# A sandwich layer on one core: expert outputs normalized in small groups behind their sums, with centred down weights

## What is computed

```python
x = x + layernorm(attention(layernorm(x)))     # linear attention, 16 heads of 8, causal sums
x = x + layernorm(ffn(layernorm(x)))

def ffn(h):                                     # 16 experts, each token goes to one
    logits  = h @ w_router.T
    scores  = sigmoid(logits) * one_hot(argmax(logits))
    gate, up = split((scores * h) @ gate_up_proj[e])
    expert  = (up * silu(gate)) @ down_proj[e]
    shared  = silu(h @ w_gate.T) * (h @ w_up.T) @ w_down.T
    return shared + expert
```

## Time and profile before

| what | value |
|---|---|
| median of the runs | 345.31 us (344.48 to 346.79, 3 runs) |
| the profiled execution | 347.56 us |
| its span, first to last instruction | 345.8 us |
| mean granted TensorE clock | 0.913 of full speed |
| busy: PE / DVE / ACT / POOL | 264.6 / 286.4 / 186.6 / 192.7 us |
| attention and the first norms | 0 to about 150 us |
| shared ffn and routing | about 150 to 235 us |
| experts, last norm and output | about 240 to 345.8 us |

### The profile page before, as it was taken

One profiled execution on the slowest core, in us unless ns is written; L12 is line 12 of the kernel. 1 busy time (PEld: TensorE's weight loads), 2 busy tenths in 40 slices (PEclk: granted clock), 3 DMA queues, 4 the chain that ended last, 5 costly groups with the idle time before them and its releaser, 6 DMA issues.

```text
span 345.8 us, 6250 instructions
## 1 busy us (share of the span) xinstructions
PE 264.6 (77%) x1465; PEld 184.2 (53%) x1465; DVE 286.4 (83%) x1138; ACT 186.6 (54%) x572; POOL 192.7 (56%) x221
## 2 busy tenths in 40 slices
PE   3459999999998995638887988821999999999000
PEld 1125556555554553325555655521999889988000
DVE  5998999999999999996998787640379999999930
ACT  2524656565665552257666664203899888885000
POOL 5056777767775863200054556570007888888870
PEclk9988999999999998967999899985899999999655
DMA  6999900000000000000011111126950101110000
GB/s 187 374 426 396 396 4 0 2 3 0 2 0 2 2 0 0 1 1 2 1 62 64 63 62 64 64 100 229 355 166 18 35 31 43 41 36 29 25 2 0
DMA packets 13668, 28.39 MB, mean 82 GB/s; under 512 B 1950, under 2 KB 10150, under 8 KB 12610
## 3 DMA queue, kind: packets, MB, share of 16 engines
q1 hardware_dynamic: 10448, 21.57, 17.1%
q0 software_dynamic: 3040, 6.37, 5.4%
q10 hardware_dynamic: 146, 0.07, 0.1%
HBM read 15.38 MB, written 13.60 MB: 84 GB/s over the span
## 4 chain that ended last, share of the span: by engine, by line
PE 39%; DVE 24%; POOL 18%; issue 12%; DMA 4%; ACT 1%; POOLq 0%; ACTq 0%; SPq 0%; another core or an unknown queue 0%; DVEq 0%
PE banks L1009 13%; POOL out L490 10%; POOL rows L484 6%; PE banks L1028 5%; PE banks L1100 5%; DVE hT L814 2%; PE banks L1037 2%; PE banks L1134 2%; POOL sorted_rows L474 2%; DVE stats L641 2%; DMA rows<-in_x 2%; PE banks L997 2%; DVE num L740 1%; DVE rows L857 1%; DVE stats L849 1%
## 5 line engine op out<-in xcount | busy, mean ns | idle before, releaser
L1009 PE MATMUL banks<-kv,upto 128*128 128x512 f32 x128 | 63.5, 621 | 1.3 <-POOL kv L449 1.3
L449 POOL TENSOR_TENSOR kv<-qk,vv 128x1024 f32<-128x1024 f32 x32 | 62.4, 1950 | 2.5
L1134 PE MATMUL banks<-xsT,w_now 128*128 128x128 f32 x376 | 52.6, 284 | 0.4 <-DVE hT_e L948 0.4
L490 POOL DMA_INDIRECT out<-rows,token_i x47 | 46.8, 997 | 9.8 <-issue 8.2
L443 POOL TENSOR_TENSOR qk<-ex,rl 128x256 f32<-128x256 f32 x32 | 23.3, 727 | 47.0 <-ACT ex L546 47.0
L1134 PEld LDWEIGHTS banks<-xsT,w_now 128*128 128x128 f32 x376 | 47.1, 197 | 1.2 <-issue 0.7
L474 POOL DMA_INDIRECT sorted_rows<-rows,slot_i x32 | 31.7, 992 | 28.7 <-DVE slot_i L804 20.7
L718 DVE TENSOR_TENSOR prod<-banks,qk 128x1024 f32<-128x1024 f32 x32 | 38.9, 1216 | 2.1 <-PE banks L1009 1.5
L740 DVE TENSOR_REDUCE num<-prod 128x128 f32<-128x1024 f32 x32 | 38.7, 1208 | 0.3 <-DVE den L735 0.3
L948 DVE TENSOR_TENSOR hT_e<-silu_e,banks 128x256 f32<-128x256 f32 x47 | 19.4, 412 | 19.8 <-ACT silu_e L623 16.1
L484 POOL TENSOR_TENSOR rows<-rows,yn 128x128 f32<-128x128 f32 x40 | 19.1, 477 | 28.0 <-DVE yn L940 26.1
(11 more groups left out here) (158 smaller groups left out, 640.0 us busy)
## 6 DMA issues: line engine op xcount, KB each, us to landing
sorted_rows<-rows SPq DMA_DIRECT2D x3, 1950.0 KB, 13.3
rows<-sorted_rows SPq DMA_DIRECT2D x11, 520.0 KB, 6.3
w_exp<-in_gate_up SPq DMA_DIRECT2D x4, 1024.0 KB, 19.7
w_exp_down<-in_down SPq DMA_DIRECT2D x4, 512.0 KB, 19.7
rows<-in_x SPq DMA_DIRECT2D x1, 1024.0 KB, 11.1
rows<-in_x SPq DMA_DIRECT2D x1, 768.0 KB, 8.4
out<-rows,token_i POOLq DMA_INDIRECT x47
sorted_rows<-rows,slot_i POOLq DMA_INDIRECT x32
```

The costliest lines, as they stand in the source:

```text
L449: nc.gpsimd.tensor_tensor(kv[:, u, :].rearrange("p (h m d) -> p h m d", h=NH, m=HD), k, v, ALU.mult).then_inc(s_kv, 1)
L490: nc.gpsimd.indirect_dma_start(out=out_rows, out_offset=bass.IndirectOffsetOnAxis(ap=token_i[:, j - 1:j], axis=0), in_=rows[:, j - 1, 0:D] ...
L1009: ins = nc.tensor.matmul(ps_s[u % 2][:, cols], upto[:], kv[:, u, cols], start=True, stop=True)
L1134: ins = nc.tensor.matmul(ps_gue[u % 2][:, c * P:(c + 1) * P], w_now[:, u % 2, c * P:(c + 1) * P], xsT[:, u % 2, :], start=True, stop=True)
```

## The change

The down weights, shared and expert, come in their untransposed layout and are multiplied on PE with `centring` = I - 1/128: two products for the shared ones at the start of attention (DVE copies them out), 32 products for the experts in eight batches around the turning of the tile ranks (ACT copies them out). With centred rows the mean needs no step of its own, so the norm takes 11 steps instead of 14 and gives one factor per row. Statistics, scratch and factors are kept for all 47 tiles. The groups of the norm are tiles 0-1, 2-3, 4-5, 6-8, 9-11, then four each, the last one three; a group's steps begin in the turn of its last tile. A row is scaled in place (`rows[:, j, D:2D]`), and the ring `yn` goes away. POOL adds the scaled row to the residual for the same 40 tiles, and scatters tile j behind the add of tile j. For the last seven DVE scales and adds in one instruction. The token numbers are made in two instructions for all tiles.

```diff
+def scale_steps(nc, series, st, width, scratch, rs):
+    yield series.done(tensor(t, mean_even, mean_even, ALU.mult))
+    yield series.done(fused(out=ve, in0=sq_even, scalar=width * EPS, in1=sq_odd, op0=ALU.add, op1=ALU.add))
+    series.wait()
...
+    yield series.done(fused(out=rs, in0=t, scalar=0.5625, in1=y, op0=ALU.add, op1=ALU.mult))
+SCALE_STEPS = 11
...
-        NORM_STEPS = [4, 3, 2, 1]
-        ADDED_BY_POOL = 4 * (QUADS - 2)
+        ENDS = [2, 4, 6, 9, 12] + list(range(16, ST, 4)) + [ST]
+        GROUPS = list(zip([0] + ENDS, ENDS))
+        TOKENS_FIRST, TOKENS_REST = 8, 12
+        ADDED_BY_POOL = 40
+        CENTRED_AT_ONCE = 2
...
         @block.gpsimd
-            for j in range(ST + 1):
+            for j in range(ST):
                 if j < ADDED_BY_POOL:
-                    r = flat(rows[:, j:j + 1, 0:D])
+                    x1 = flat(rows[:, j:j + 1, 0:D])
                     pool.wait_ge(s_yn, j + 1)
-                    nc.gpsimd.tensor_tensor(r, r, yn[:, j % 4, :], ALU.add).then_inc(s_fin, 1)
-                if j > 0:
-                    if j <= ADDED_BY_POOL:
-                        pool.wait_ge(s_fin, j)
-                    else:
-                        pool.wait_ge(s_fin_last, j - ADDED_BY_POOL)
-                    nc.gpsimd.indirect_dma_start(
-                        out=out_rows, out_offset=bass.IndirectOffsetOnAxis(ap=token_i[:, j - 1:j], axis=0),
-                        in_=rows[:, j - 1, 0:D], in_offset=None,
+                    nc.gpsimd.tensor_tensor(x1, x1, flat(rows[:, j:j + 1, D:2 * D]), ALU.add).then_inc(s_fin, 1)
+                    pool.wait_ge(s_fin, j + 1)
+                else:
+                    pool.wait_ge(s_fin_last, j + 1 - ADDED_BY_POOL)
+                if j in (0, TOKENS_FIRST):
+                    pool.wait_ge(s_token, 1 + (j > 0))
+                nc.gpsimd.indirect_dma_start(
+                    out=out_rows, out_offset=bass.IndirectOffsetOnAxis(ap=token_i[:, j:j + 1], axis=0),
+                    in_=rows[:, j, 0:D], in_offset=None,
...
         @block.scalar
+            for n in range(E // CENTRED_AT_ONCE):
+                act.wait_ge(s_turned_e, n + 1)
+                nc.scalar.copy(w_exp_down[:, CENTRED_AT_ONCE * n:CENTRED_AT_ONCE * (n + 1), :, :].rearrange(
+                    "p e c d -> p (e c d)"), ps_centred[n % 3][:]).then_inc(s_centred_e, 1)
             act.wait_ge(s_experts, 1)
...
         @block.vector
             last.then_inc(s_norm1, 1)
+            nc.vector.tensor_tensor(centring[:], ident[:], neg_mean[:], ALU.add).then_inc(s_centring, 1)
...
             left_of_bias(1)
+            dve.wait_ge(s_turned_d, 1)
+            nc.vector.tensor_copy(w_d[:].rearrange("p c d -> p (c d)"), ps_s[1][:, 0:FC * D]).then_inc(s_centred_d, 1)
...
+            def scale_row(i):
+                dve.wait_ge(s_series3, SCALE_STEPS * (GROUP_OF[i] + 1))
+                if i < ADDED_BY_POOL:
+                    nc.vector.tensor_scalar(r, r, rstd3[:, i:i + 1], None, ALU.mult).then_inc(s_yn, 1)
+                else:
+                    nc.vector.scalar_tensor_tensor(out=x1, in0=r, scalar=rstd3[:, i:i + 1], in1=x1,
+                                                   op0=ALU.mult, op1=ALU.add).then_inc(s_fin_last, 1)
+            for j in range(-2, ST + 1):
+                many, most = begun in (1, 2, 3), begun == 1
                 if live(j + 2, ST):
...
                     nc.vector.tensor_tensor(hT_e[:, u % 2, :], silu_e[:, u % 2, :], ps_gue[u % 2][:, F:2 * F],
+                chain_steps(1 + many)
                 if live(j, ST):
...
                     nc.vector.tensor_tensor(r, ps_ye[u % 2][:, 0:D], r, ALU.add).then_inc(s_sum, 1)
+                chain_steps(1 + most)
+                if scaled < ST and begun > GROUP_OF[scaled] + (left > 0):
+                    scale_row(scaled)
+                    scaled += 1
+                chain_steps(1 + many)
...
+                if live(j, ST):
+                    dve.wait_ge(s_sum, j + 1)
+                    nc.vector.bn_stats(stats3[:, j, :], r).then_inc(s_stats3, 1)
+                chain_steps(1 + most)
+                if begun < len(GROUPS) and j + 1 == GROUPS[begun][1]:
+                    chain_steps(left)
+                    chain, left, begun = scales(begun), SCALE_STEPS, begun + 1
+                    chain_steps(1)
...
         @block.tensor
             def step1(t, u):
+                if t == 0:
+                    pe.wait_ge(s_centring, 1)
+                    pe.wait_ge(s_w2, 16)
+                    for c in range(FC):
+                        ins = nc.tensor.matmul(ps_s[1][:, c * D:(c + 1) * D], w_down[:, c * P:(c + 1) * P], centring[:],
...
+            def centre(n):
+                pe.wait_ge(s_wexp, 16 * (E // 4) * 2)
+                at_least(pe, s_centred_e, n - 2)
+                for k in range(CENTRED_AT_ONCE * FC):
+                    e, c = CENTRED_AT_ONCE * n + k // FC, k % FC
+                    ins = nc.tensor.matmul(ps_centred[n % 3][:, k * D:(k + 1) * D], w_exp_out[:, e, c * P:(c + 1) * P],
+                                           centring[:], start=True, stop=True)
+                ins.then_inc(s_turned_e, 1)
+            centre(0)
+            centre(1)
             pe.wait_ge(s_tile_rank, 1)
...
+            for n in range(2, E // CENTRED_AT_ONCE):
+                centre(n)
             pe.wait_ge(s_experts, 1)
-            pe.wait_ge(s_wexp, 16 * (E // 4) * 2)
+            pe.wait_ge(s_centred_e, E // CENTRED_AT_ONCE)
```

More of the change, by code:

```diff
@@ L366, in build @@
         s_series3 = sem("norm_steps3")
-        s_yn = sem("ffn_normed")
+        s_yn = sem("ffn_scaled")
+        s_token = sem("tokens_ready")
         s_fin = sem("output_ready")
@@ L913, in _ @@
             nc.vector.tensor_scalar(tile_expert[:], tile_expert[:], E - 1, None, ALU.bitwise_and).then_inc(s_experts, 1)
[L917 to L944, removed]
@@ new lines, in scales @@
+            def scales(g):
+                c = slice(*GROUPS[g])
+                norm = Series(dve, s_series3, SCALE_STEPS * g)
+                dve.wait_ge(s_stats3, GROUPS[g][1])
+                yield from scale_steps(nc, norm, [stats3[:, c, k] for k in (1, 2, 5)], D,
+                                       [scratch3[:, k, c] for k in range(3)], rstd3[:, c])
+            def scale_row(i):
+                x1, r = flat(rows[:, tiles(i), 0:D]), flat(rows[:, tiles(i), D:2 * D])
+                dve.wait_ge(s_series3, SCALE_STEPS * (GROUP_OF[i] + 1))
[4 more added lines that the diff above has]
+                                                   op0=ALU.mult, op1=ALU.add).then_inc(s_fin_last, 1)
@@ new lines, in tokens, with chain_steps @@
+            def tokens(j0, j1):
+                dve.wait_ge(s_loaded, LOADED[j1 - 1])
+                nc.vector.tensor_scalar(token_i[:, j0:j1], rows[:, j0:j1, TOKEN], -1.0, float(NTOK), ALU.mult, ALU.add
+                                        ).then_inc(s_token, 1)
+            begun, scaled = 0, 0
+            chain = iter(())
+            left = 0
+            def chain_steps(count):
+                nonlocal left
+                for _ in range(count):
+                    if left:
+                        next(chain)
+                        left -= 1
@@ L949, in step3 @@
                                             ALU.mult).then_inc(s_he, 1)
[L950 to L958, removed]
-                    nc.vector.tensor_tensor(flat(rows[:, i, 0:D]), flat(rows[:, i, 0:D]), yn[:, u, :],
-                                            ALU.add).then_inc(s_fin_last, 1)
+                chain_steps(1 + many)
                 if live(j, ST):
@@ L965, in step3 @@
                     nc.vector.tensor_tensor(r, ps_ye[u % 2][:, 0:D], r, ALU.add).then_inc(s_sum, 1)
[L966 to L984 removed]
+                chain_steps(1 + most)
[3 more added lines that the diff above has]
+                chain_steps(1 + many)
+                if j == 0:
+                    tokens(0, TOKENS_FIRST)
+                if j == TOKENS_REST:
+                    tokens(TOKENS_FIRST, ST)
+                if live(j, ST):
[6 more added lines that the diff above has]
+                    chain_steps(1)
+            while scaled < ST:
+                if begun > GROUP_OF[scaled] + (left > 0):
+                    scale_row(scaled)
+                    scaled += 1
+                chain_steps(2)
         @block.tensor
```

72 lines of the change are left out of this document (46 added, 26 removed).

## The result

| | kernel before | changed kernel |
|---|---|---|
| median | 346.05 us (344.48 to 347.23, 4 runs) | 364.31 us (362.87 to 364.77, 4 runs) |
| ratio to before | 1 | 1.0505, interval 1.046 to 1.055 |
| profiled execution, its span | 347.56, 345.8 us | 364.77, 362.9 us |
| first `xs` of the last stage | 239.31 us | 239.76 us |
| POOL's first add | 258.33 us | 253.71 us |

The changed kernel is 5% slower. The ratio is the recorded one; the quotient of the two medians shown is 1.053, inside its interval. In the profiled executions the last scatter ends 17.2 us later.

What follows compares the result with a forecast made beforehand. POOL was taken to bound the last stage: 253.5 + 0.2 + 90.8 + 9.0 ends the last scatter at 353.5, +15.8 us, so 363.4 for the profiled execution, 361.1 on the median's scale; range 356 to 366.

Steps and rivals of the forecast that it cites:

- POOL's turn: Last stage, per tile: add 0.48, gap 0.78, scatter 1.00, step 0.01, together 2.27 us for each of 40 tiles.
- preparation: Some 0.75 us a scatter needs after the sequencer's last waiting instruction; taken as 0.72, idle on POOL in the new order.
- the free wait: Rival: scatter's wait for its own add costs nothing, gap 0.17, turn 1.66, 338.0 us; chance 0.06.
- The rival with the preparation under the wait: Scatter is prepared while waiting for its own add: gap 0.36, turn 1.85, 344.3 us, no measurable change; chance 0.09.
- The break-even gap of 0.385: Gap between POOL's add and its scatter, at a turn of 1.875, below which the kernel is not slower.
- The start: POOL's first add in the last stage: 5.1 us earlier by small groups and fewer steps, 0.3 later by shared weights, 253.5.
- The sum: End of the last scatter's work: first add, pause, 40 turns and seven scatters give 353.5 instead of 337.7, +15.8 us.
- the pause: POOL may wait once for DVE's group 1 near the stage's start: 0 to 0.5 us, taken as 0.2.
- The seven scatters without an add: Last seven rows, added by DVE: POOL's scatters go on at 1.28 us each, 9.0 us together.
- DVE under cover: DVE's steady turn in the last stage, at most 1.5 us, stays covered by POOL; last sum near 317, end some 5 later.
- Centring: Expert weights' products on PE end near 235.5, hidden before `xs` at 239.31; possible clock gain up to 1.5 us, none taken.
- The shared weights: Start of attention: DVE's new copy may delay PE's product of 25.29 by 0.3 us, bounds 0 and 0.6.

Runs made afterwards that it cites:

- experiment 4: Changed kernel with the scatter's bound put into a register once ahead of the loop, so the wait sits on the scatter: 344.4 us, ratio 0.9960.
- experiment 6: Kernel before with scatter j directly behind add j and the bound kept in one register: 346.95 us, ratio 1.0035.
- experiment 8: Changed kernel with the bound kept in one register, plus a register instruction without a wait between add and wait: 345.11 us, ratio 0.9983.
- experiment 3: Changed kernel with DVE scaling and adding all 47 rows in one instruction each, POOL only scattering: 334.27 us, ratio 0.9675.

## Why the prediction was right

**POOL's turn.** Forecast 2.27 us, measured 2.29: the gap is 0.79 instead of 0.78 and the step from scatter to add 0.02 instead of 0.01. Behind the sequencer's instruction the changed kernel has 0.73 bare, where the routing stage had 0.72. That was the mechanism of the forecast, and the runs bear it out further than the prediction could: in all eight kernels with a register instruction ahead of their scatters, no scatter starts less than 0.757 us behind its own, counted off one by one. What the chip does in this stretch no row shows; "preparation" is only a name for it. The Trainium skill, "DMA: Bandwidth & Descriptors", section "Anatomy of one DMA — SWDGE (gpsimd) path", has about 50 ns for the sequencer's dispatch; as a price of this wait, for which the prediction tried it, the trace doesn't agree with it. The rival that follows from it is the free wait (the second of the three, not the third, as the prediction says): a scatter right behind its own add starts 0.27 us or more behind it in every run.

**The rival with the preparation under the wait** did not come about, but its mechanism exists. It was priced at a gap of 0.36 and 344.3 us; experiment 4 has 0.28 and 344.4 us. That the two times agree is luck: the gap is smaller, and POOL loses most of the difference in waits for DVE that the price left out. What decides between the two is where the wait stands. On the scatter itself, only 0.28 us follow the add; on an instruction of the sequencer ahead of it, 0.79. The Trainium skill, "Perfetto Trace Analysis", section "DMA Instruction — SWDGE (GPSIMD)", draws decoding first and the wait behind it, in a queue; experiments 4, 6 and 8 agree with that order, and the changed kernel shows that it doesn't hold for a wait that the sequencer has to sit out first. The prediction looked at the right line of the old trace, where the register instruction carries the wait. The break-even gap of 0.385 was not tested closely: 0.79 is slower and 0.28 (experiments 4 and 8) is not. By that sum 0.28 would have gained 4.2 us; the stage gained 1.5 in experiment 4, because of the same waits. So by these runs the break-even lies somewhat lower.

**The start.** Forecast for the first add 253.5, with 5.1 us won by the groups and 0.3 lost to the shared weights. The first add comes at 253.71. Counted from `xs`, it is 13.9 us behind it instead of 19.0: 5.1 won. That the time itself is met within 0.2 is in part luck, as `xs` comes up to 3 us earlier in other executions. The timeline of POOL at the start:

```profile
253.71 0.45 POOL L524 TENSOR_TENSOR rows<-rows 128x128 f32<-128x128 f32 x1 [19.60 <-DVE rows L981]
255.01 1.01 POOL L530 DMA_INDIRECT out<-rows,token_i  x1 [0.85 <-POOL rows L524]
...
258.76 0.45 POOL L524 TENSOR_TENSOR rows<-rows 128x128 f32<-128x128 f32 x1 [0.44 <-DVE rows L981]
```

POOL waits once more for DVE, 0.44 us for tile 2, where 0.2 was taken and 0 to 0.5 allowed. After that it never waits, as said.

**The sum.** Forecast end of the last scatter 353.5, measured 354.85. The 1.35 us that are missing: 0.2 from the first add, 0.24 from the pause, 0.9 from forty turns (91.7 instead of 90.8; one scatter, that of tile 37, came 0.29 late by itself). The seven scatters without an add took 9.0 as forecast. So the profiled execution took 364.77 instead of 363.4. On the scale of the medians the forecast was 361.1 and the result 364.31. Beyond the 1.35 us this is because the profiled execution of before lay 2.25 above the median shown and that of the changed kernel only 0.46 above its own: the front of the kernel differs that much from one execution to another.

**DVE under cover.** Forecast to be done near 322. The last DVE group ends at 321.6, by its timeline:

```profile
320.50 1.12 DVE L983 SCALAR_TENSOR_TENSOR rows<-rows,rstd 128x128 f32<-128x128 f32 x3
```

The chain of waits ends on POOL, behind 0.30 between two scatters as in the earlier trace rows:

```profile
353.56 0.30 issue
353.87 0.98 POOL out L530
```

DVE is done 33 us ahead of POOL, so nothing that the change saves on it in the steady state could count.

**Centring.** Forecast to end near 235.5, hidden, with no gain of clock. The timelines of PE and ACT:

```profile
229.27 5.63 PE L1188 MATMUL banks<-centring,w_exp_out 128*128 128x128 f32 x48
...
234.93 0.58 ACT L642 COPY w_exp_down<-banks 128x512 f32<-128x512 f32 x1 [0.31 <-PE banks L1188]
239.76 0.49 ACT L658 ACTIVATE xs<-rows 128x128 f32<-128x128 f32 x1 [4.24 <-SPq L458]
...
241.75 1.93 PE L1211 MATMUL banks<-xsT,w_now 128*128 128x128 f32 x8
```

The last copy ends at 235.51; ACT then sits idle for 4.24 us until the sorted rows are back, so the work is hidden. The first tile's products take 1.93 us, at a granted clock of 0.50, the lower level, as before (1.94, also at 0.50): no gain.

**The shared weights.** Taken at 0.3, with 0 to 0.6. In the chain near the start PE's product now begins at 25.96 and not at 25.29, behind DVE's carry:

```profile
25.60 0.22 DVE carry L760
25.83 0.14 issue
25.96 0.98 PE banks L1093
```

That is 0.67 later, just above the upper bound; but as equal programs differ by more than that at the start of the last stage, how much of it reaches the end stays open.

## What to carry to other kernels

When one queue both makes a row and sends it, leave a tile of distance between the two, or see to it that the wait stands on the transfer itself and not on an instruction that is issued for it ahead (here a register for the bound check, kept outside the loop): the distance was worth 21 us, the wait's place 18 of them. Ask of every fixed latency in the old trace what covers it, and of every new order whether the cover is still there. And ask whether the engine that has the transfers must have the arithmetic too: here, with the additions on DVE, the same change is 3% faster than before.

## What was not expected of the hardware

- The place of a wait counts: 0.79 us from the end of an add, POOL's or DVE's, to its indirect scatter if the wait stands on the sequencer's register instruction; 0.28 if on the scatter, also with a register instruction that waits for nothing and is passed early. An add and the scatter of an earlier row behind it are 0.17 apart, two scatters in a row 0.30.
- In the changed kernel DVE's plain scaling is on average no cheaper than scaling with the addition in it is in experiment 3, where POOL adds nothing. The groups of DVE from 262 to 312 us, first the changed kernel, then experiment 3:

```profile
L981 DVE TENSOR_SCALAR rows<-rows,rstd 128x128 f32<-128x128 f32 x33 | 12.4, 375 | 0.3
```

```profile
L983 DVE SCALAR_TENSOR_TENSOR rows<-rows,rstd 128x128 f32<-128x128 f32 x32 | 11.1, 347 | 0.3
```

One scaling takes 375 ns on average, from 271 to 748; scaling and addition in one take 347, from 339 to 355 (up to 395 over the whole stage). In experiment 4, where POOL adds as well, the same scaling takes 317 on average. The difference is made by a few long ones, and their ends lie close to an end on POOL. The longest:

```profile
262.28 1.00 POOL L530 DMA_INDIRECT out<-rows,token_i  x1 [0.79 <-POOL rows L524]
262.58 0.75 DVE L981 TENSOR_SCALAR rows<-rows,rstd 128x128 f32<-128x128 f32 x1
```

The scatter ends at 263.28 and the scaling at 263.33. All 11 scalings of the changed kernel over 0.4 us begin within an instruction of POOL and end 0.05 us behind it where it is a scatter (four) and 0.09 to 0.10 where it is an add (seven). But 11 others that begin within one stay short, so what decides is open. The Trainium skill, "GPSIMD Engine Reference", section "1. Specifications", says that GpSimd shares its memory interfaces with VectorE, with contention for some kinds of VectorE instructions; the rows agree with such contention, without proving it, and which kind this scaling is no row shows. So in the changed kernel giving the addition to POOL took no time off DVE.
